# A recommender tower of three compressed-interaction layers: a twelfth split pair, layer 2's split products a slot behind its plain ones, and the transposes moved

## What is computed

```python
x0 = xk = e                                   # 2048 x 39 x 16
for idx, (W, b) in enumerate(params):         # W: 39 x K x 128, K = 39, 64, 64
    z = relu(einsum('bhd,bkd,hks->bsd', x0, xk, W) + b[None, :, None])
    if idx != 2:
        xk = z[:, :64]; direct.append(z[:, 64:])
    else:
        direct.append(z)
logit = sum(concatenate(direct, axis=1), axis=-1)          # 2048 x 256
h = relu(concatenate([logit, dense_ctx], 1) @ W_top1 + b_top1)
h = relu(h @ W_top2 + b_top2)
y = h @ W_top3
```

## Time and profile before

| what | us |
|---|---|
| median of three runs | 2543.55 |
| the profiled execution's own time | 2545.02 |
| span of its trace | 2543.1 |
| before the first matmul of layer 0 | 77.35 |
| start of the last chunk's layer 1 on TensorE | 2432.21 |
| start of the dense tower on TensorE | 2469.42 |
| TensorE matmuls busy | 2432.8 (96%) |
| VectorE busy | 2268.7 (89%) |
| GpSimd busy | 1557.9 (61%) |
| ScalarE busy | 1175.5 (46%) |

### The profile page before, as it was taken

The page is one execution under the profiler, slowest core; times in us unless marked ns, Lnnn a source line. Parts: engine busy times, 40 slices in busy tenths (PEclk is TensorE's granted clock), DMA queues, the critical chain, the costliest instruction groups (busy, mean ns, idle before and its releaser), DMA issues.

```text
span 2543.1 us, 25999 instructions
## 1 busy us (share of the span) xinstructions
PE 2432.8 (96%) x7712; PEld 1423.5 (56%) x7712; DVE 2268.7 (89%) x1356; ACT 1175.5 (46%) x1414; POOL 1557.9 (61%) x1029
## 2 busy tenths in 40 slices
PE   0599999999999999999999999999999999999999
PEld 0265555556555555555555565555556555555553
DVE  0599999999999999999999999999999999999960
ACT  0244444445454444545444444444444444445442
POOL 6476667667666766766676666667666766743240
PEclk9899999999999999999999999999999999999999
DMA  2986777777677777867777776787777677766610
GB/s 69 246 211 180 199 207 202 180 217 214 176 198 205 207 178 215 209 182 197 209 206 177 217 206 190 190 211 210 178 207 205 200 184 213 207 182 194 195 30 0
DMA packets 262712, 477.02 MB, mean 188 GB/s; under 512 B 19500, under 2 KB 37788, under 8 KB 262614
## 3 DMA queue, kind: packets, MB, share of 16 engines
q1 hardware_dynamic: 141766, 271.07, 38.9%
q10 hardware_dynamic: 100480, 200.29, 28.5%
q0 software_dynamic: 20448, 5.45, 1.4%
HBM read 468.99 MB, written 7.74 MB: 187 GB/s over the span
## 4 chain that ended last, share of the span: by engine, by line
PE 73%; POOL 10%; DVE 6%; issue 4%; DMA 4%; ACT 2%; SPq 0%; POOLq 0%; DVEq 0%; ACTq 0%
PE z L693 37%; PE z L716 33%; POOL emb L352 5%; DVE prod L418 4%; POOL pair_lo L211 4%; DMA emb<-in_tbl,idx 3%; PE xk L775 1%; PE z L775 1%; DMA x_pairs<-x_transposed 1%; ACT pair_hi L532 1%; POOL half_parts L207 1%; DVE pair_lo L211 1%; PE turned L674 1%; DVE logit L448 1%; ACT xk L542 0%
## 5 line engine op out<-in xcount | busy, mean ns | idle before, releaser
L418 DVE TENSOR_TENSOR prod<-x_pairs,xk 128x2048 f32<-128x2048 f32 x640 | 1436.4, 2284 | 75.2 <-PE z L716 46.9
L693 PE MATMUL z<-prod,w_plain 128*128 128x512 f32 (+2 forms) x2944 | 1383.1, 594 | 40.5 <-DVE prod L418 40.5
L532 ACT CAST pair_hi<-prod 128x1024 fp32r<-128x1024 f32 x703 | 735.4, 1046 | 1085.2 <-PE z L716 793.6
L211 POOL TENSOR_TENSOR pair_lo<-prod,pair_hi 128x1024 fp32r<-128x1024 f32 x320 | 764.1, 2388 | 638.3 <-ACT pair_hi L532 621.7
L693 PEld LDWEIGHTS z<-prod,w_plain 128*128 128x128 f32 (+2 forms) x2944 | 555.4, 189 | 474.1 <-issue 394.9
L352 POOL DMA_INDIRECT emb<-in_tbl,idx x624 | 701.3, 1124 | 184.0 <-issue 173.7
L716 PE MATMUL z<-pair_hi,w_lo 128*128 128x512 f32 (+1 forms) x1408 | 786.6, 559 | 2.3 <-DVE pair_lo L211 1.7
L716 PE MATMUL z<-pair_hi,w_hi 128*128 128x512 f32 (+1 forms) x1408 | 555.7, 395 | 0.0
L716 PE MATMUL z<-pair_lo,w_hi 128*128 128x512 f32 (+1 forms) x1408 | 555.1, 394 | 0.0
L211 DVE TENSOR_TENSOR pair_lo<-prod,pair_hi 128x1024 fp32r<-128x1024 f32 (+1 forms) x384 | 468.5, 1220 | 48.7 <-ACT pair_hi L532 48.7
L716 PEld LDWEIGHTS z<-pair_hi,w_lo 128*128 128x128 f32 (+1 forms) x1408 | 265.2, 188 | 297.2 <-POOL pair_lo L211 135.8
(11 more groups left out here) (50 smaller groups left out, 566.5 us busy)
## 6 DMA issues: line engine op xcount, KB each, us to landing
x_pairs<-x_transposed SPq DMA_DIRECT2D x64, 2432.0 KB, 16.9
x_pairs<-x_transposed ACTq DMA_DIRECT2D x64, 2432.0 KB, 19.3
x_diag<-x_transposed SPq DMA_DIRECT2D x128, 546.0 KB
x_diag<-x_transposed ACTq DMA_DIRECT2D x64, 546.0 KB
x_pairs<-x_transposed SPq DMA_DIRECT2D x64, 256.0 KB, 20.4
emb<-in_tbl,idx POOLq DMA_INDIRECT x624, 6.3
x_diag<-x_transposed SPq DMA_DIRECT2D x128, 78.0 KB
x_transposed<-stage SPq DMA_DIRECT2D x32, 156.0 KB
```

What stands on the lines that cost most here:

```text
L211: engine.tensor_tensor(pair_lo[0:rows, pair % PAIR_RING], held[0:rows, at:at + 2, :], pair_hi[0:rows, pair % PAIR_RING].bitcast(F32), ALU. ...
L418: nc.vector.tensor_tensor(prod[0:rows, pos % RING, 0:n, :], a, xk.unsqueeze(1).broadcast_to([rows, n, N]), ALU.mult).then_inc(prod_ready, 1)
L532: nc.scalar.copy(pair_hi[0:rows, pair % PAIR_RING], held[:, at:at + 2, :]).then_inc(hi_ready, 1)
L693: ins = nc.tensor.matmul(z[n][:], w, held[0:rows, i, :], start=(k == 0 and i == plain[0]), stop=(k == last_slot and not here and i == plai ...
```

## The change

- **Twelve pairs.** Layer 0 splits a second pair (tiles 2 and 3 of its first slot), so it has three plain tiles left in place of five.
- **Who subtracts.** The second pair of layer 1 goes from VectorE to GpSimd. The other low parts of layer 1 stay on VectorE, but they read a second copy of the high part, which ScalarE writes to PSUM (`hi_copy`, and `direct01` for the half tile). VectorE no longer skips the subtraction behind slot 1 of layer 1.
- **Rings.** High and low parts lie in a ring of six tiles (`PARTS`), three pairs in place of two.
- **PSUM.** `hi_copy` takes two banks and shares them with the transposes; `direct01` moves from SBUF to PSUM; `xk0` shares the bank of `xk2`, so `xk2` waits for layer 0's products (`act.wait_ge(prod_ready, slot + SL0)`).
- **TensorE's order.** In layer 2 the split tiles of slot k come behind the plain tiles of slot k+1 (`BEHIND`). Layer 0 waits for both its slots, runs all its plain tiles, then its two pairs, and frees both slots together. The transposes stand behind the plain tiles of layer 2's slot 1, no longer between layers 1 and 0, and ScalarE fills `stage` behind `direct_0` of that layer.
- **Gathers.** GpSimd has 20 fields of the next group ahead in place of 30, and gathers between the low part of layer 1 and those of layer 2.
- **Sums.** `logit01` and `logit2` keep a window of 128 columns. SyncE stores each window once a group (`store_window`), at the head of its lists for chunks 0 and 1, and the tower loads the sums back, in ten loads in place of six.

```diff
-SPLITS = {0: [(0, 0, 2)],
-          1: [(0, 0, 2), (1, 0, 2), (2, 0, 2), (2, 3, 1), (3, 0, 2), (4, 0, 2)],
-          2: [(0, 0, 2), (1, 0, 2), (2, 0, 2), (2, 3, 1), (3, 0, 2), (4, 0, 2)]}
-EARLY = {1: 4, 2: 4}
+V, G = "VectorE", "GpSimd"
+SPLITS = {0: [(0, 0, 2, V), (0, 2, 2, V)],
+          1: [(0, 0, 2, V), (1, 0, 2, G), (2, 0, 2, V), (2, 3, 1, V), (3, 0, 2, V), (4, 0, 2, V)],
+          2: [(0, 0, 2, G), (1, 0, 2, G), (2, 0, 2, G), (2, 3, 1, G), (3, 0, 2, G), (4, 0, 2, G)]}
+EARLY = {1: 5, 2: 4}
+BEHIND = {1: False, 2: True}
...
+                    if c == 0:
+                        sp.wait_ge(summed01, bt * CHUNKS + 1)
+                        store_window(0, bt)
+                    if c == 1:
+                        sp.wait_ge(summed2, bt * CHUNKS + 2)
+                        store_window(1, bt)
                     if c == 2 and not last:
                         store_group(bt + 1)
...
+                    if n and who == V:
+                        copies = [s for s in SPLITS[n][0:i] if s[3] == V]
+                        if m == 1:
+                            nc.scalar.copy(direct01[0:HALF].bitcast(F32R), held[0:HALF, at, :]
+                                           ).then_inc(hi_copied, 1)
+                        else:
...
+                            nc.scalar.copy(hi_copy[:, 0:m, :].bitcast(F32R), held[:, at:at + m, :]
+                                           ).then_inc(hi_copied, 1)
...
+                        round_splits(0, slice(0, None), slot, pos, used_by, chunk)
+
+                        act.wait_ge(prod_ready, slot + SL0)
                     hand_on(1, xk2, b1_sb, slot)
...
-                    if c == 1 and not last:
-                        fill_stage(bt + 1)
...
-                        act.wait_ge(summed01, chunk + 1)
+                        act.wait_ge(summed01, chunk + 2)
                         direct_0()
-                        pair = round_splits(SPLITS[2][EARLY[2]:], P, slot, pos, pair, held_by)
+                        if c == 1 and not last:
+                            fill_stage(bt + 1)
+
+                            act.wait_ge(stage_ready, 2 * (bt + 2))
+                        round_splits(2, slice(EARLY[2], None), slot, pos, used_by, chunk)
...
+                    for i in plain:
+                        plain_part(n, t, i, held, k == 0 and i == plain[0], False)
+                    if k == turn_at:
+                        transpose_group(turn)
+                    if not BEHIND[n]:
+                        split_parts(n, k, lows)
+                    elif k > 0:
+                        split_parts(n, k - 1, lows)
+                if BEHIND[n]:
+                    split_parts(n, last_slot, lows)
```

More of the change, by code:

```diff
@@ L78 @@
 NB = 512
-assert CB < NB < B and len(SPLITS[0]) == 1
+assert CB < NB < B and all(k == 0 for k, _, _, _ in SPLITS[0])
 def top_order():
@@ L420, in product @@
                                         ALU.mult).then_inc(prod_ready, 1)
-            def products(steps, split, pair, next_chunk):
-                late = []
-                for n, k, copies, xk, slot, pos in steps:
-                    if n == k == 0:
-                        dve.wait_ge(xk0_ready, next_chunk + 1)
-                    first, rows, tiles = (FIRST_TILE[k], P, TX) if n else (L0_FIRST[k], R0, T0)
-                    product(slot, pos, copies[0:rows, first:min(first + QUAD, tiles), :], xk[0:rows])
-                    if (n, k) != (1, 1):
-                        for item in late:
-                            split, pair = subtract(item, split, pair)
-                        late = []
-                    late += [(n, pos, at, m) for at_slot, at, m in SPLITS[n] if at_slot == k]
-                for item in late:
-                    split, pair = subtract(item, split, pair)
@@ new lines, in splits_of, with products @@
+            def splits_of(n, pos, slot, chunk):
+                copies, here = lows(1, V) if n == 2 else 0, []
+                for s, place in zip(SPLITS[n], PLACES[n]):
+                    copy = chunk * COPIES_C + copies if n else None
+                    copies += s[3] == V
+                    if s[0] == slot:
+                        here.append((n, pos, copy, place, *s))
+                return here
+            def products(n, copies, xk, slot, pos, late, split, chunk):
+                first_tile, rows, tiles = (FIRST_TILE, P, TX) if n else (L0_FIRST, R0, T0)
+                for k, first in enumerate(first_tile):
+                    product(slot + k, pos + k, copies[0:rows, first:min(first + QUAD, tiles), :],
+                            xk[0:rows])
+                    split = subtract(late, split)
+                    late = splits_of(n, pos, k, chunk)
+                return late, split
@@ L456, in sum2 @@
                                         z[2][:].rearrange("p (d b) -> p b d", b=CB),
                                         AXIS.X, ALU.add).then_inc(summed2, 1)
-            def layer(n, copies, xk, slot, pos):
-                return [(n, k, copies, xk, slot + k, pos + k) for k in range(SLX if n else SL0)]
-            products(layer(0, x0_diag, xk0, 0, 0), 0, 0, 0)
+            dve.wait_ge(xk0_ready, 1)
+            late, split = products(0, x0_diag, xk0, 0, 0, [], 0, 0)
+            subtract(late, split)
@@ L490, in group @@
                         if k == 1:
-                            sum01(chunk)
-                    pair = pair_after + PAIRS[2]
+                            sum01(bt, c)
+                        split = subtract(late, split)
+                        late = splits_of(2, pos, k, chunk)
+                    subtract(late, split)
             with dve.Fori(0, GROUPS - 1) as bt:
@@ L601, in group @@
             def group(bt, last):
-                pair = PAIRS[0]
                 before = SL0 + bt * CHUNKS * SLC
-                held_by = [before - SLX + k for k, _, n in SPLITS[2] if n == 2]
+                used_by = {place + i: before - SLX + k for (k, _, m, _), place
+                           in zip(SPLITS[2], PLACES[2]) if m > 1 for i in range(m)}
                 for c in range(CHUNKS):
@@ L677, in transpose_group, with plain_part @@
                         ins.then_inc(turned_ready, 1)
-            def layer(n, slot, pos, split, pair):
-                whole, hi, lo, splits = w_plain[n], w_hi[n], w_lo[n], SPLITS[n]
-                first_tile = FIRST_TILE if n else L0_FIRST
-                last_slot = len(first_tile) - 1
-                for k, t in enumerate(first_tile):
+            def plain_part(n, t, i, held, first, last):
+                rows = P if n else R0_LAST if t + i == T0 - 1 else R0
+                w = w_plain[n][0:rows, PLAIN_TILES[n].index(t + i), :]
+                return nc.tensor.matmul(z[n][:], w, held[0:rows, i, :], start=first, stop=last)
```

320 lines of the change are left out of this document (191 added, 129 removed).

## The result

The changed kernel took 2706.2 us, the median of four runs (2702.7 to 2712.6), against 2546.0 us before (2541.5 to 2548.5): 1.063 times as long, 95% interval 1.061 to 1.066. The forecast was 2492 us, range 2481 to 2530, with 0.10 for slower. It was wrong by 214 us and on the wrong side.

What follows compares the result with a forecast made beforehand. Bound by TensorE's work plus a small coupling: 2543.1 - 61 (loop) + 3 (restarts) + 8 (bands) + 0.6 (head) - 2 (tail) = 2491.7 us of span, about 2492 us; range 2481 to 2530.

Steps and rivals of the forecast that it cites:

- Store and bands: Chunk 2's later store delays the x0_diag bands: issue +5.0, landed +16.9, needed by +16.5; 8 us lost in all.
- the upper bound: Bands taking 16.9 us, as SyncE's half of x0_pairs does: landed at +21.9, 5.4 us lost a group.
- rival 2: Bands on SyncE's queue come late beside ScalarE's 2432 KB; each us past +16.5 costs 15: 2565 us, chance 0.10.
- TensorE's work: Layer 0: two plain tiles become six rounded products, 0.32 us less a chunk, a floor of 35.71 us.
- Layer 2 a slot behind: TensorE's waits for GpSimd's low parts in layer 2 all go, 0.65 us a chunk.
- VectorE and ScalarE: VectorE needs 35.6 us a chunk, under 35.71; low parts from PSUM 1.22 us, ScalarE copies 1.0, sum01 0.69.
- rival 3: Low parts from PSUM or copies cost 0.3 us more, VectorE becomes the bound: 2535 to 2550 us, chance 0.07.
- Transposes: Moved into layer 2, they cost a group 0.93 us plus up to 0.3, without waiting for gathers.
- Window stores, head and tail: Window stores cost nothing; the head gets 0.6 us later; the last chunk saves about 2 us.

Runs made afterwards that it cites:

- e3: Changed kernel with ScalarE's half of x0_pairs issued late in chunk 2, behind its copy of xk0; 2603.1 us.
- e1: Changed kernel with SyncE issuing the bands of x0_diag ahead of the four stores in chunk 2, on chip 1; 2498.8 us, 0.982 of before.
- g2: The kernel of e1 again, unedited, on chip 3; 2536.0 us, 0.996 of before.
- g1: The changed kernel again, without an edit, on chip 3; 2695.1 us, 1.058 of before.
- i2: Kernel of e1, both pairs in layer 0, with GpSimd's index load ahead of layer 2's low parts, chip 1; 2485.1 us, 0.976 of before.
- i1: Kernel of h3 with GpSimd's index load in chunk 1 ahead of layer 2's low parts, on chip 1; 2503.6 us, 0.983 of before.
- h3: Kernel of h1 with one split pair in layer 0, the ring advanced all the same, on chip 4; 2522.2 us, 0.991 of before.
- h1: The kernel of e1 again, unedited, on chip 4; 2548.1 us, 1.001 of before.
- e2: Changed kernel with transposes back between layers 1 and 0, stage filled earlier, 30 fields gathered ahead; 2585.6 us, 1.017 of before.
- e4: Changed kernel with gathers back behind layer 2's low parts, the wait for the last chunk's gathers, 30 fields ahead; 3473.2 us, 1.365 of before.
- f4: Kernel of e1 with one split pair in layer 0 in place of two, the ring one pair short; 2616.8 us.
- g4: Kernel of e1 with GpSimd's gathers held until ScalarE has made all high parts of layer 1, on chip 3; 2724.3 us.
- h2: Kernel of h1 without the gathers of chunks 0 and 3, 20 of a group's 39; 2516.8 us.

## Why the prediction was wrong

**Store and bands** is the step that failed. Its issue time was right (+5.2 for +5.0) and its deadline too. Wrong was the 11.9 us from issue to use, taken from the head with the words "I take the lower, nearer in size". "With nothing beside it" was too strong even there: in these 11.9 us SyncE's queue moved 1.28 MB, ScalarE's 0.64, its own band, and the gathers 0.08. But no bulk was ahead of the bands. Here 2432 KB had been issued on ScalarE's queue 2.7 us ahead of the bands, and it took 21.5 us. e3 shows both sides: without that transfer 11.8 us. Even the upper bound (landed at +21.9) was too low; the bands were used at +26.7, since the transfer held up the store ahead of them too, until about +13. The step's rule, each us past +16.5 costs 15, then gives 15 x 10 = 150 us; measured on chip 3, 159.

The argument against rival 2, that two queues side by side moved 2432 KB in 16.9 us, was read from transfers that the two queues had issued within 0.1 to 0.6 us of each other. Here one started 2.7 us earlier with 2432 KB against four small stores. The rule of the Trainium skill, "DMA: Bandwidth & Descriptors", section on queues, rings and completion order, by which each DMA engine goes round-robin between queues with work, was the right warning. But the trace shows less than an even share for SyncE's queue: nothing at all for 5 us, then 0.26 MB beside 0.77 in the next 4. Rival 2 had the right mechanism and a price half of the real one (+73 us on the forecast, where it cost 159).

**The late releases** were in no step and no rival. They are the 37 us between e1 and g2 (3 of them the chips' difference for the kernel before), and in the changed kernel what chunk 0 and more than half of what chunk 3 have too much. Nothing in the trace of before pointed there. The balance: 2492 + 7 (e1) + 37 (late releases, chip 3) + 159 (bands) = 2695 us, as g1; the first measurement was 11 us above. The 7 us of e1 are small by luck: the late gathers cost it 1.0 us in each chunk 3, 15 us, which no step had, and the 8 us put down for the bands it didn't pay. i2 has neither cost and took 2485.1 us, where the forecast without the 8 us is 2484. So on a chip without late releases the rest of the sum came out.

**TensorE's work** was right: 35.80 us for 35.71 in an undisturbed chunk, and the twelfth pair 0.32 for 0.32. In the whole the twelfth pair gained 18 us on chip 1 (i1 and i2) and lost 26 us on chip 4 (h3 and h1). The pairs of runs differ in the place of the index load too, so that the chip alone makes the difference isn't shown.

**Layer 2 a slot behind** was right in kind, 0.55 for 0.65 us a chunk. The forecast took all waits as gone. The weight loads' waits for GpSimd fell from 135.8 us only to 65.7 us in the changed kernel. With the bands ahead of the store they were 34.4 us on chip 1 (e1) and 90.4 us with late releases (g2), in one and the same kernel:

```profile
PEld z L796 <- POOL lo_parts L251: 34.4, 56, 0.9
```

```profile
PEld z L796 <- POOL lo_parts L251: 90.4, 189, 1.4
```

In i2, with early indices, the list of waits has none. So the forecast's wait goes, and what came back came with the late gathers and the late releases.

**VectorE and ScalarE** were right: 1.21 us for 1.22, 1.01 for 1.0, `sum01` 0.68 for 0.69. By the Trainium skill, "VectorE: DVE Perf Modes", section on the TRN2 errata, a PSUM source would cost more; the trace again shows no surcharge: 1210 ns with the high part in PSUM, 1216 from SBUF (117 partitions), 1220 in the kernel before (128). VectorE had 1.2 us of idle time in a chunk of 35.8, so rival 3 is out.

**Transposes** were right: a group of i2 is 144.08 - 4 x 35.80 = 0.9 us longer than four plain chunks (0.93 to 1.2 was forecast), with no wait for gathers but the first group's. The 0.9 us fall into chunks 1 and 2, since VectorE, by whose products the chunks are counted, is ahead of TensorE.

**Window stores, head and tail**: the first product of layer 1 came 1.7 us earlier, not 0.6 later, and from the last chunk's first product to the end it was 118.5 us for 118.8, 0.3 less and not 2. All small.

## What to carry to other kernels

When a small transfer moves behind another in time, look at every queue for what is issued in the us before it: a large DMA that is already running on a second queue can hold a short chain up for more than half of its own length (here 21.5 us in place of 11.8, beside a transfer of some 16). Put the small transfer that someone waits for ahead of the store and the bulk; the reorder of one line was worth 159 us, twenty times what the forecast had put down for the bands (8 us). Compare variants only on the same chip. And where a test reorders a ring or a queue, check first what else now waits behind it: four of my runs (e2, e4, f4, g4) measured their own side effect.

## What was unexpected in the hardware

- The same kernel took 2498.8 us on one chip and 2536.0 and 2548.1 us on two others, while the kernel before differed by 3 us. The difference is in semaphore updates of TensorE that arrive late, by 3.6 and 3.7 us where shown above, while gathers land beside a large transfer; without gathers (h2) or with them behind the transfer (g4) they are in time. Why chips differ is open. Only the chips with late updates also miss updates in their traces (below), so it isn't excluded that the recording of the trace has a part in it; no run tests this.
- A trace of chips 2 to 4 can be told at sight: the page has no time to landing for `x0_pairs`, since many updates are missing from it. g4's lacks it too, so it marks the chip and not the delay. First e1 on chip 1, then g2 on chip 3:

```profile
x_pairs<-x_transposed SPq DMA_DIRECT2D x64, 2432.0 KB, 16.6
```

```profile
x_pairs<-x_transposed SPq DMA_DIRECT2D x64, 2432.0 KB
```

- Two queues don't share evenly: SyncE's moved nothing for 5 us while ScalarE's moved 1.03 MB.
